# An audio tower's inputs laid out in kernel() with the contracted dimension on partitions

## The reference

```python
# tokenizer: pairs of rows -> one token (16 x 128 tokens of 256)
xb = x.reshape(B, L // 2, 2, D)
x = einsum('btki,oik->bto', xb, conv_w) + conv_b
x = x + xb.mean(axis=2)
x = layernorm(x) * ln_gamma + ln_beta
# layer 0: h += attention(layernorm(h)), window of 64 keys, 16 heads
q, k, v = n @ Wq.T, n @ Wk.T, n @ Wv.T ;  out @ Wo.T
# layer 0: h += shared MLP + 2 of 16 experts, capacity 320
# layer 1: h += causal attention (w_qkv, w_out), 16 heads
# layer 1: h += 3 of 64 experts, capacity 128
h = gelu(buf @ w1 + b1) ;  y = h @ w2 + b2
```

## Time and profile before

| | us |
|---|---|
| median of 3 runs | 1224.52 |
| lowest, highest | 1220.88, 1227.47 |
| the profiled execution | 1219.43 |
| its span, first to last instruction | 1217.70 |
| tokenizer, attention and routing of layer 0 | 0 to 235 |
| shared MLP and 16 experts of layer 0 | 235 to 512 |
| attention and routing of layer 1 | 512 to 742 |
| 64 experts of layer 1 | 742 to 1217 |

### The profile page before, as it was taken

How to read it: one execution, slowest core, us unless ns; L and a number is a source line. 1 busy time by engine, 2 the same in 40 slices (tenths; PEclk the granted TensorE clock), 3 DMA queues, 4 the chain that set the end, 5 groups by cost and what they waited for, 6 DMA issues and landing times.

```text
span 1217.7 us, 23672 instructions
## 1 busy us (share of the span) xinstructions
PE 1093.2 (90%) x7360; PEld 895.7 (74%) x7360; DVE 506.2 (42%) x2647; ACT 518.1 (43%) x1896; POOL 323.2 (27%) x319
## 2 busy tenths in 40 slices
PE   6999988688999999779889736999999999999996
PEld 5787776455666665457667626999999999999995
DVE  4689887421322322248888641222222222222221
ACT  1998888201111111079989702333333333333331
POOL 4144343301333344001424222222222222222222
PEclk9999998699999999989999857999999999999999
DMA  9623200005566663390100026999999999999990
GB/s 320 245 106 110 110 27 26 26 23 155 126 158 126 148 139 42 115 367 11 37 13 19 9 76 249 325 308 313 319 318 316 303 315 311 318 317 304 319 315 10
DMA packets 153390, 218.95 MB, mean 180 GB/s; under 512 B 15214, under 2 KB 125253, under 8 KB 152800
## 3 DMA queue, kind: packets, MB, share of 16 engines
q1 hardware_dynamic: 134368, 203.40, 48.9%
q0 software_dynamic: 18944, 14.62, 7.1%
HBM read 184.74 MB, written 43.09 MB: 187 GB/s over the span
## 4 chain that ended last, share of the span: by engine, by line
PE 62%; DVE 14%; issue 8%; DMA 7%; POOL 5%; ACT 4%; POOLq 0%; SPq 0%; DVEq 0%; ACTq 0%
PE bank L1111 19%; PE bank L1124 18%; PE bank L1051 5%; POOL rows L656 4%; PE bank L1008 4%; PE bank L1062 3%; DMA rows<-ffn_in,scatter_i 2%; DVE probs L1468 2%; ACT probs L1192 2%; PE bank L1018 2%; DMA early<-rows 2%; DMA stream<-arena,slot_token 2%; PE bank L799 1%; PE bank L778 1%; PE bank L1097 1%
## 5 line engine op out<-in xcount | busy, mean ns | idle before, releaser
L1369 ACT ACTIVATE dhidT<-bank,b1T 128x128 f32<-128x128 f32 x512 | 146.3, 369 | 308.3 <-PE bank L1111 308.2
L1111 PE MATMUL bank<-probsT,arena 128*128 128x128 f32 x2048 | 240.6, 276 | 0.0
L1111 PEld LDWEIGHTS bank<-probsT,arena 128*128 128x128 f32 x2048 | 235.1, 193 | 0.3 <-DVE probsT L1803 0.2
L1124 PE MATMUL bank<-arena,dhidT 128*128 128x256 f32 x1024 | 231.5, 379 | 0.0
L1124 PEld LDWEIGHTS bank<-arena,dhidT 128*128 128x128 f32 x1024 | 189.8, 190 | 23.2
L1192 ACT ACTIVATE probs<-probs,neg_max 128x128 f32<-128x128 f32 x512 | 197.8, 393 | 1.7 <-DVE neg_max L1468 1.4
L720 POOL DMA_INDIRECT out<-probsT,slot_token x64 | 98.6, 1541 | 375.5 <-DMA out<-probsT,slot_token 327.7
L1820 DVE TENSOR_TENSOR probsT<-bank,b_wide 128x256 f32<-128x256 f32 x64 | 27.2, 424 | 346.6 <-PE bank L1124 346.6
L656 POOL DMA_INDIRECT rows<-ffn_in,scatter_i x80 | 79.9, 998 | 206.3 <-DVE scatter_i L1608 176.7
L691 POOL DMA_INDIRECT stream<-arena,slot_token x48 | 72.5, 1511 | 172.0 <-DVE arena L1774 160.1
L1468 DVE CUSTOM_DVE_ANT_0 probs<-bank,mask 128x128 f32<-128x128 f32 x512 | 112.6, 283 | 11.2 <-PE bank L820 11.1
(11 more groups left out here) (162 smaller groups left out, 1333.6 us busy)
## 6 DMA issues: line engine op xcount, KB each, us to landing
arena<-L_ffn_w SPq DMA_DIRECT2D x128, 1024.0 KB, 7.2
rows<-zeros SPq DMA_DIRECT2D x13, 1024.0 KB, 8.3
drows<-rows SPq DMA_DIRECT2D x64, 132.0 KB, 7.4
arena<-L_ffn_w_gate SPq DMA_DIRECT2D x16, 352.0 KB, 3.8
arena<-L_ffn_w_up SPq DMA_DIRECT2D x16, 352.0 KB, 4.8
early<-rows SPq DMA_DIRECT2D x16, 264.0 KB, 2.7
early<-x SPq DMA_DIRECT2D x8, 512.0 KB, 4.5
arena<-L_ffn_w_down SPq DMA_DIRECT2D x16, 256.0 KB, 3.3
```

The lines of the kernel that those rows point to most:

```text
L1111: mm = pe.matmul(bank[2 + 2 * (u % 2) + half][:, jj * P:(jj + 1) * P], w1_sb[u][:, c, j * P:(j + 1) * P], drowsT[:, u % 2, c, :], start=c ...
L1124: last_ = pe.matmul(bank[6 + u % 2][:, 0:D], dhidT[:, u % 2, j, :], w2_sb[u][:, j, :], start=j == 0, stop=j == J1 - 1)
L1369: last_ = act.activation(dhidT[:, u % 2, j, :], bank[2 + 2 * (u % 2) + half][:, jj * P:(jj + 1) * P], ACT.Gelu, bias=b1T[:, j, bass.ds(e, 1)])
```

## The change

kernel() lays out on the host x, the tokenizer's weights, the four projections and b1 so that the contracted dimension is on the partitions. The kernel loads them straight to where the turned copies were: conv_wT, wT0, b1T, and xT. The jobs X0 and X1, the steps turn_x, prep_job, keep_weights and keep_xT, and the four staging buffers are gone. xT has two buffers, of which one takes x_in's place, and the load of pair i waits until the convolution of pair i - 2 is written. b1 is loaded after the second x. The waits for the router loads move from the head of body 0 to route (PE) and take_logits (DVE) of the first pair.

```diff
-        X0, X1, CONV0, CONV1, TURN, Q, K, V, INVERSE, SPREAD, OUT, TURN_FFN, ROUTE, COUNT, PROBS = range(15)
+        CONV0, CONV1, TURN, Q, K, V, INVERSE, SPREAD, OUT, TURN_FFN, ROUTE, COUNT, PROBS = range(13)
-        JOB_ORDER = (((PROBS + 2, -1), (PROBS + 3, -1), (TURN_FFN, -2), (X1, 2), (X0, 2), (ROUTE, -2), (CONV1, 2), (PROBS + 4, -1),
+        JOB_ORDER = (((PROBS + 2, -1), (PROBS + 3, -1), (TURN_FFN, -2), (ROUTE, -2), (CONV1, 2), (PROBS + 4, -1),
...
-            sp.dma_start(conv_raw, a["L0_tok_conv_w"].rearrange("(m o) i k -> o m (i k)", m=2)).then_inc(conv_in, 16)
-            load_x(0, True)
+            def load_x(i):
+
+                if i > 1:
+                    wait_written(sp, L0, (i - 2, CONV0), (i - 2, CONV1))
+                sp.dma_start(xT[i % 2], a["x"][i]).then_inc(L0.x_loaded[i % 2], 16)
+
+
+            sp.dma_start(conv_wT[:, :, :], a["L0_tok_conv_w"]).then_inc(conv_in, 16)
+            load_x(0)
             for w, name in enumerate(("Wq", "Wk", "Wv", "Wo")):
-                sp.dma_start(w_raw[:, w], a[f"L0_attn_{name}"].rearrange("(m o) d -> o m d", m=2)).then_inc(raw_in, 16)
-            sp.dma_start(b1_raw, a["L1_ffn_b1"]).then_inc(raw_in, 16)
+                sp.dma_start(wT0[:, w, :, :], a[f"L0_attn_{name}"]).then_inc(turned_in, 16)
...
-            load_x(1, False)
+            load_x(1)
+            sp.dma_start(b1T[:, :, :], a["L1_ffn_b1"]).then_inc(turned_in, 16)
...
-            def turn_x(i, t):
-                wait(pe, L0.x_loaded, 16 * (i + 1))
-                bk, full = new_job(L0, i, X0 + t)
+            def conv(i, t):
+                if i == 0 and t == 1:
+                    pe.wait_ge(conv_ready, 1)
+                pe.wait_ge(L0.x_loaded[i % 2], 16 * (i // 2 + 1))
+                bk, full = new_job(L0, i, CONV0 + t)
                 for c in range(2 * DC):
-                    last = pe.transpose(bk[:, c * P:(c + 1) * P], x_in[:, t, c * P:(c + 1) * P], ident[:, :])
+                    last = pe.matmul(bk[:, 0:D], xT[i % 2][:, t, c, :], conv_wT[:, c, :], start=c == 0, stop=c == 2 * DC - 1)
                 last.then_inc(full, 1)
...
                 if L is L0 and i == 0:
                     pe.wait_ge(const_p, 19)
-                    pe.wait_ge(prep_free, prep[0])
+                    pe.wait_ge(turned_in, 16 * 5)
...
-                if i == 0:
-                    keep_weights(2, len(places))
...
+    x = x.reshape(b // 2, 2, tokens // 2, 2 * d // P, P)
+    arrays["x"] = np.ascontiguousarray(x.transpose(0, 4, 1, 3, 2))
```

More of the change, by code:

```diff
@@ L118, in __init__ @@
         if n == 0:
-            self.x_loaded = sem("x_loaded")
+            self.x_loaded = [sem(f"x_loaded{b}") for b in range(2)]
             self.tok_normed = sem("tok_normed")
@@ L731, in _ @@
             pe.wait_ge(const_p, 2)
[L732 to L746, removed]
-                              for c in range(DC) for m in range(2)])
-            def turn_weights():
-                pe.wait_ge(raw_in, 16 * 5)
-                for w in range(4):
-                    prep_job([((c * 2 + m) * P, w_raw[:, w, m, c * P:(c + 1) * P], P)
-                              for c in range(DC) for m in range(2)])
-                prep_job([(j * NE1, b1_raw[:, j * P:(j + 1) * P], NE1) for j in range(J1)])
             def new_job(L, i, k, *read):
@@ L764, in new_job @@
                 return job_bank[b], L.job_full[b]
-            def turn_x(i, t):
-                wait(pe, L0.x_loaded, 16 * (i + 1))
-                bk, full = new_job(L0, i, X0 + t)
+            def conv(i, t):
[3 more added lines that the diff above has]
+                bk, full = new_job(L0, i, CONV0 + t)
                 for c in range(2 * DC):
-                    last = pe.transpose(bk[:, c * P:(c + 1) * P], x_in[:, t, c * P:(c + 1) * P], ident[:, :])
+                    last = pe.matmul(bk[:, 0:D], xT[i % 2][:, t, c, :], conv_wT[:, c, :], start=c == 0, stop=c == 2 * DC - 1)
                 last.then_inc(full, 1)
-            def conv(i, t):
-                if i == 0:
-                    pe.wait_ge(conv_ready, 1)
-                bk, full = new_job(L0, i, CONV0 + t, (i, X0 + t))
-                for c in range(2 * DC):
-                    last = pe.matmul(bk[:, 0:D], xT[:, t, c, :], conv_wT[:, c, :], start=c == 0, stop=c == 2 * DC - 1)
-                last.then_inc(full, 1)
-                if i == 0 and t == 0:
-                    turn_weights()
             def turn_normed(L, i):
@@ L880, in route @@
             def route(L, i):
+                if L is L0 and i == 0:
+                    pe.wait_ge(router_in, 16 * ROUTER_LOADS)
                 bk, full = new_job(L, i, ROUTE, (i, TURN_FFN))
@@ L1377, in _ @@
         def _(dve):
-            places = [conv_wT[:, 2 * k:2 * k + 2, :] for k in range(2)] + [wT0[:, w, :, :] for w in range(4)] + [b1T[:, :, :]]
-            def keep_weights(first, end):
-                for n in range(first, end):
-                    dve.wait_ge(prep_full, n + 1)
-                    dve.tensor_copy(places[n], prep_bank[n % len(prep_bank)][:, :].rearrange("p (a b) -> p a b", a=places[n].shape[1])).then_inc(prep_free, 1)
-            keep_weights(0, 2)
             dve.wait_ge(const_p, 2)
-            dve.wait_ge(prep_free, 2)
+            dve.wait_ge(conv_in, 16)
             for k in range(2):
@@ L1508, in take_logits @@
             def take_logits(L, i):
+                if L is L0 and i == 0:
+                    dve.wait_ge(router_in, 16 * ROUTER_LOADS)
                 E = L.E
@@ L1853 @@
     arrays = {name: np.ascontiguousarray(inputs[name]) for name in NAMES}
+    x = arrays["x"]
+    b, tokens, d = x.shape
+    x = x.reshape(b // 2, 2, tokens // 2, 2 * d // P, P)
+    arrays["x"] = np.ascontiguousarray(x.transpose(0, 4, 1, 3, 2))
+    w = arrays["L0_tok_conv_w"]
+    arrays["L0_tok_conv_w"] = np.ascontiguousarray(w.transpose(2, 1, 0).reshape(2 * d // P, P, d).transpose(1, 0, 2))
+    for name in ("L0_attn_Wq", "L0_attn_Wk", "L0_attn_Wv", "L0_attn_Wo", "L1_ffn_b1"):
+        w = arrays[name].T
+        arrays[name] = np.ascontiguousarray(w.reshape(w.shape[0] // P, P, w.shape[1]).transpose(1, 0, 2))
     a = {name: nc.dram_tensor(name, arrays[name].shape, F32, kind="ExternalInput").ap() for name in NAMES}
-    b, tokens, d = arrays["x"].shape
     out = nc.dram_tensor("out", [b, tokens // 2, d], F32, kind="ExternalOutput").ap()
```

47 lines of the change are left out of this document (9 added, 38 removed).

## The result

| | before | after |
|---|---|---|
| median of 20 runs, us | 1221.45 | 1226.28 |
| lowest, highest | 1216.79, 1227.87 | 1221.42, 1234.50 |
| ratio, 95% interval | | 1.0034, 1.0018 to 1.0050 |
| profiled execution, its span | 1219.43, 1217.7 | 1224.77, 1222.8 |
| first scores of layer 0 | 30.83 | 29.26 |

The change costs 0.34%, about 4 us; 1221.4 was predicted and 1226.28 measured. In the two traces the kernel is 2.1 us ahead at 66 us and 3.4 us behind at 239 us. So the question isn't why too little was gained at the start, but what takes 5.6 us from bodies that have lost work.

A forecast was written before the change was run, and what follows sets the result against it. The prediction took a DVE, POOL, DVE loop to set the steady bodies' period. Gains of 2.0 (start), 0, 0.3 (body 1) and 0.76 (bodies 2 to 5), 3.1 us, took 1224.52 to 1221.4; range 1214.5 to 1226.5.

The forecast's parts named there:

- rival C: Bodies 2 to 5: PE's idle grows, the clock falls, 4.5 us more per body, 18 in all, 1240 us; chance 0.06.
- the part that can move: Start and first seven of layer 0's twelve attention passes: only the first 142 us can move, gains carried to the end.
- The start: Program start to first scores: 2.54 us earlier by the first normalisation, less 0.55 for the clock, 2.0 us in all.
- The five copies: DVE's weight copies between first statistics and normalisation: removing them gives about 1.6 us.
- The clock: Start: the clock falls before the transposes of normed tokens, costing 0.55 us; extremes 2.35 lost or 1.7 won.
- sign of a wrong start: First normalisation on DVE: expected at about 14.2 us; later than 15 us would show the start forecast wrong.
- that head start: First convolution without the copies and transposes ahead: worth nothing by itself, since the first mix waits for bias rows.
- Body 1: Second attention body: gains 0.3 of 1.07 us; the rest becomes a bank wait before the third probability transposes.
- Bodies 2 to 5: Steady attention bodies: DVE passes the convolution 0.19 us sooner, the rest waits for POOL; 0.76 us in all.
- rival A: Whole touched part: PE is the bound, each removed transpose paid in full, 7.7 to 9.4 us, 1215 to 1217; chance 0.22.
- Loads and moved waits: x loads issued earlier, waits for router loads and turned weights moved: all costed at 0.
- Rival B: Start and bodies: nothing arrives, low clock, bank wait and POOL take the gains, 1224.3 us; chance 0.17.

The follow-up runs named there:

- e12_after_again: The changed kernel run once more, unaltered, for a second trace: 1225.80 us, ratio 1.0026 to the kernel before.
- e3: The changed kernel plus eight identity transposes in each of bodies 0 to 5, near the removed x transposes, behind a wait: 1227.60 us, ratio 1.0042.
- e11: The changed kernel plus identity transposes in all long TensorE waits of layer 0's attention and at layer 1's head: 1213.75 us, ratio 0.9930.
- e8_before_fill: The kernel before plus eight identity transposes in the wait ahead of the FFN input's, bodies 2 to 5: 1224.12 us, ratio 1.0004.
- e5_fill_exact: The changed kernel plus eight identity transposes in the very places of the x transposes, bodies 0 to 5: 1219.92 us, ratio 0.9979.
- e10_dose5: The changed kernel plus five identity transposes in TensorE's wait ahead of the FFN input's, bodies 2 to 5: 1221.73 us, ratio 0.9993.
- e2_x_only: The changed kernel with weights and b1 turned on the chip again, only x laid out on the host: 1226.71 us, ratio 1.0036.
- e9_start_only: The changed kernel plus 44 identity transposes in TensorE's wait ahead of the first normed tokens: 1222.30 us, ratio 0.9996.

## Why the prediction was wrong, point by point

**The step that failed** is the dismissal of rival C. The rival named the mechanism and the place: PE's idle grows, the clock falls in bodies 2 to 5, the chain from the FFN transposes to the convolution stretches, and more than 1 us of loss in a body outweighs all gains. It got 6 chances in 100 on this argument: "the clock is 1.00 in these bodies, and PE stays above 20 us busy in 24". So the sum took the clock in bodies 2 to 5 as given and put its loss at nothing. The first half read a level that held with the x transposes in place as a property of the stage; what they did for the clock was asked for the start alone. Measured were two falls, 2.69 us each. The second half was true: PE is 22.73 of 25 us busy in a body that kept its clock, and the next one falls. A busy share of a whole body doesn't say where in it PE idles. The prediction also ended the part that can move at 142 us, with seven of the bodies that make tokens; there are eight, and the second fall (143.0 to 149.9 us) lies in the eighth.

**Its price** was off as well: 4.5 us in each of four bodies, 18 in all. Measured 2.69 in each of two. The chain stretched by 2.83 us (9.30 against 6.47), not by 5.5: the clock falls only after the FFN transposes, is back before the convolution's end, and between these PE also waits for DVE's maxima, which the clock doesn't touch. And of bodies 2 to 5 no two neighbours fell in any trace, so half of them paid at most. With 2 x 2.69 in place of 18, C's own sum is 1224.5 - 2.3 + 5.4 = 1227.6 and not 1240. That the measured 1226.28 lies inside the range is no credit to it: the median of the kernel before was 1221.45 over twenty runs and not the 1224.52 of three, so the same 1226.28 means a loss of 4.8 us, where the range allowed 2.

**The start**: 2.54 us forecast by the first normalisation, 2.31 measured (14.42 against 16.73). The statistics came 0.66 us earlier, not 0.94: the bias rows were in 0.43 earlier (11.22 for 11.65), where 0.67 was taken, and the second mix lost its 0.27 us wait, as forecast. The five copies gave their 1.65. The clock was to take back 0.55, and the fall was to come before the normed transposes: it did (they took 1.09 us, and K and Q 5.77 against 5.41), 0.8 us. First scores 1.57 us earlier for the forecast 2.0. That is the best case of the kernel, not the rule: in its second trace the first normalisation comes at 15.36, beyond the 15 us that the prediction named as the sign of a wrong start, and the first scores at 30.60. The next part has the reason.

**The first convolution.** The Trainium skill (TensorE: Matmul & The Clock Gate, What's actually happening) was set aside with the words that the trace doesn't agree at the program's start. It does. The first convolution took 5.73 us for the 3.72 of the same product later, although the granted clock column reads 1.00 there. The column reads 1.00 where the trace has no record of the clock: the first record is at 9.9 us in after and at 11.7 in e12_after_again. I took this for a level; the durations decide. In the trace before it could have been seen: the eight x transposes at 6.52 us took 1.68 us there, and the next eight, at 15.11 us, took 1.09. In after it cost nearly nothing, because the bias rows arrive at 11.2 us and the first convolution was over at 11.51. In e12_after_again, the same kernel, it cost 1 us:

```profile
11.13 0.42 DVE L1375 TENSOR_TENSOR early<-bank,conv_b 128x256 f32<-128x256 f32 x1 [3.62 <-DMA beta<-L_tok_ln_beta]
12.55 0.42 DVE L1375 TENSOR_TENSOR early<-bank,conv_b 128x256 f32<-128x256 f32 x1 [1.00 <-PE bank L740]
...
15.36 0.73 DVE L1360 TENSOR_SCALAR early<-early,moments,rstd 128x256 f32<-128x256 f32 x2 [1.24 <-POOL rstd L626]
```

Of the ten traces that share this start (after, e12 and e3 to e11 without e8_before_fill), seven have such a wait of the second mix, 0.40 to 1.51 us, and the first normalisation comes between 14.39 and 15.55. The prediction's "that head start is worth nothing by itself" left out that a convolution which starts before the clock is up may end later than the bias rows come. The steady bodies go the same way: the Trainium skill's rule is that throttled is the default and activity lifts it. With eight transposes less in each, two of them fell to 1.2 GHz (after), and with eight back none did (e5_fill_exact). So a change that takes activity away has to be priced with it everywhere, not at the start alone.

**Body 1**: the new wait for the bank was forecast at about 0.7 us ahead of the third group of probability transposes, ended by DVE's mix. It is there with 0.62:

```profile
50.14 0.63 PE L789 MATMUL bank<-ident,probs 128*128 128x128 f32 x4 [0.62 <-DVE early L1375]
```

From the first scores (1.57 us early) to the FFN transposes of body 2 (2.13 early) bodies 0 and 1 gained 0.56, forecast 0.3.

**Bodies 2 to 5**: the gain of 0.19 each is right where the clock holds (0.29 and 0.13), and so is that DVE and not PE leads there: rival A's period of 23.3 was seen in no kernel. With falls kept away the gains are there up to the end of attention, 2.44 us in e10_dose5. Loads and moved waits were costed at nothing. One wait for a load is new, 0.96 us of the second convolution for x at 12.46, and it holds nobody up: that convolution started at 16.45 before. No wait for the router loads or for the turned weights appears. Rival B (1224.3) isn't what happened either: the gain arrived, to 66 us, and was then lost.

## What to carry to other kernels

Work that an engine does in the shadow of another may be free in time and still hold TensorE's clock up. Before removing matmuls or transposes from a loop that TensorE doesn't lead, price the case that its granted clock falls: stretch the chain through it at the low level and see who waits. If it falls, a few transposes of a constant put ahead of TensorE's longest wait gave the clock back here at no cost, provided they stand before the wait and not behind it, and only where there is a wait; and in a kernel whose TensorE waits at stage borders the same fill is worth more than the removed work was (0.7% against none that the runs can tell).

## What the runs showed of the hardware

- In a loop in which TensorE is over 90% busy, idle stretches of 1.76 and 0.28 us close together were followed by a fall to 1.2 GHz that lasted 6.8 us (91.8 to 98.7), TensorE working throughout. Body 3 of e2_x_only, with 1.77 and 0.28 us, kept its clock. With four transposes between these two waits, and four more behind the scores (e5_fill_exact, idle 1.57 us), or five ahead of them (e10_dose5, idle 1.23 us), it didn't fall.
- Three traces (after, e9_start_only, e12_after_again) fall in bodies 3 and 5 and not in 4; each fall starts 1.4 to 1.8 us behind the start of the FFN input's transposes. In after body 6 falls right behind body 5.
- At the program's start TensorE worked slowly until some 10 us in after, while the profile's clock column read 1.00: 5.73 us against 3.72 for sixteen matmuls.
- What decides which body falls stays open: between bodies 4 and 5 of e2_x_only (idle 1.41 us and no fall, idle 1.39 us and a fall), between its body 3 and that of after, and in body 6, which falls in three of fourteen traces. Nor was it tried whether another activity than transposes of the identity does as well.
